# A hybrid transformer kernel on one core: the rotary fold, the first squares and the activation tables of its layer loop are moved

## The reference

```python
for i in range(6):                                   # DEPTH
    x = attn_layer(shift_tokens(x), Wqkv[i], q_scale[i], k_scale[i], Wo[i]) + x
    x = ffn_layer(shift_tokens(x), ln_g[i], ln_b[i], W1[i], b1[i], W2[i], b2[i]) + x

# attn_layer: 16 heads of 64, window 32, on n = 2048 tokens
q = l2norm(q) * qs                                   # divide by the root of the sum of squares
k = l2norm(k) * ksc
q = q * cos * scale + rotate_half(q) * sin * scale   # rotary position tables
k = k * cos * inv + rotate_half(k) * sin * inv
out = local_attention(q, k, v)                       # softmax over 64 keys
# ffn_layer: 128 -> 2 x 341 -> 128
a, gate = jnp.split(xn @ W1 + b1, 2, -1)
return a * jax.nn.gelu(gate, approximate=False) @ W2 + b2
```

## Time and profile before

| | us |
|---|---|
| median of 3 runs | 5192.34 (5176.46 to 5194.83) |
| the profiled execution | 5198.14 |
| its span, first to last instruction | 5196.3 |
| PE busy | 4459.6 (86%) |
| DVE busy | 3876.7 (75%) |
| ACT busy | 3326.2 (64%) |
| POOL busy | 2834.6 (55%) |

### The profile page before, as it was taken

One profiled execution on the slowest core, in us unless ns is written; L12 is line 12 of the kernel. 1 busy time (PEld: TensorE's weight loads), 2 busy tenths in 40 slices (PEclk: granted clock), 3 DMA queues, 4 the chain that ended last, 5 costly groups with the idle time before them and its releaser, 6 DMA issues. The chain is left out here.

```text
span 5196.3 us, 198441 instructions
## 1 busy us (share of the span) xinstructions
PE 4459.6 (86%) x70382; PEld 2776.0 (53%) x70382; DVE 3876.7 (75%) x8099; ACT 3326.2 (64%) x11398; POOL 2834.6 (55%) x2110
## 2 busy tenths in 40 slices
PE   5999999598897988989889756988989889798896
PEld 1333332266565665656656534665656656566565
DVE  7888787387786877868768545877868778687785
ACT  1777777476585775857758413766757667476584
POOL 3000000376675766757667404766757667576674
PEclk6999999899998999999999876999989999899998
DMA  0000000233233232332332302233333322323233
GB/s 13 1 2 2 2 1 1 76 78 86 73 79 87 74 85 76 78 90 73 86 78 78 84 14 86 77 86 78 79 82 79 86 73 77 87 77 85 73 79 97
DMA packets 415347, 340.20 MB, mean 65 GB/s; under 512 B 170607, under 2 KB 312469, under 8 KB 412693
## 3 DMA queue, kind: packets, MB, share of 16 engines
q1 hardware_dynamic: 413972, 332.35, 24.1%
q10 hardware_dynamic: 768, 0.02, 0.0%
HBM read 100.42 MB, written 30.41 MB: 25 GB/s over the span
## 5 line engine op out<-in xcount | busy, mean ns | idle before, releaser
L946 POOL TENSOR_TENSOR g_rn<-g_ss,g_minus_half 128x8 f32<-128x8 f32 x378 | 718.6, 1901 | 394.9 <-DVE g_ss L1151 392.7
L946 POOL TENSOR_TENSOR f_rn<-f_ss,f_minus_half 128x8 f32<-128x8 f32 x378 | 718.3, 1900 | 388.8 <-DVE f_ss L1151 384.3
L427 DVE TENSOR_REDUCE a_maxima<-a_max 128x1 f32<-128x512 f32 x1024 | 651.5, 685 | 150.2 <-PE a_max L541 144.0
L351 ACT ACTIVATE a_pex<-a_scores 128x512 f32<-128x512 f32 x1024 | 531.9, 607 | 162.9 <-PE a_scores L550 162.9
L1014 ACT ACTIVATE f_ex<-f_bank,f_nmx 128x64 f32<-128x64 f32 x1536 | 461.3, 314 | 137.6 <-DVE f_nmx L1144 136.8
L1014 ACT ACTIVATE g_ex<-g_bank,g_nmx 128x64 f32<-128x64 f32 x1536 | 461.4, 314 | 132.2 <-DVE g_nmx L1144 131.4
L951 POOL TENSOR_TENSOR g_qr<-g_t 128x512 f32<-128x512 f32 x384 | 493.3, 1285 | 11.8 <-DVE g_t L1124 11.8
L951 POOL TENSOR_TENSOR f_qr<-f_t 128x512 f32<-128x512 f32 x384 | 492.1, 1282 | 13.0 <-DVE f_t L1124 13.0
L1254 PE MATMUL g_bank<-g_wqkv,g_xT 128*128 128x512 f32 x744 | 437.5, 673 | 69.5 <-DVE g_qh L1138 49.7
L1254 PE MATMUL f_bank<-f_wqkv,f_xT 128*128 128x512 f32 x744 | 431.9, 665 | 71.9 <-DVE f_qh L1138 51.8
L282 POOL COPY a_v_head<-a_v_all 128x128 f32 (+1 forms) x16 | 4.6, 289 | 697.9 <-PE a_sums L559 697.9
(11 more groups left out here) (252 smaller groups left out, 11214.6 us busy)
## 6 DMA issues: line engine op xcount, KB each, us to landing
f_vw<-f_vt SPq DMA_DIRECT2D x576, 128.0 KB
g_vw<-g_vt SPq DMA_DIRECT2D x576, 128.0 KB
f_vw<-f_vt SPq DMA_DIRECT2D x384, 64.0 KB
g_vw<-g_vt SPq DMA_DIRECT2D x384, 64.0 KB
f_wqkv<-in_f_Wqkv_dram SPq DMA_DIRECT2D x7, 1536.0 KB, 8.1
g_wqkv<-in_f_Wqkv_dram SPq DMA_DIRECT2D x7, 1536.0 KB, 7.8
f_xs<-xf SPq DMA_DIRECT2D x196, 32.0 KB, 1.8
g_xs<-xf SPq DMA_DIRECT2D x196, 32.0 KB, 1.8
```

Of the source, the lines that this page charges most:

```text
L351: act.activation(pex[:, kt % 2, i % NG, :], ps_s[i % 3][:], ACT.Exp).then_inc(act_ex, 1)
L427: dve.tensor_reduce(maxima[:, m // 4, m % 4:m % 4 + 1], ps_max[m % 3][:], AX.X, ALU.max).then_inc(dv_max, 1)
L946: pool.tensor_tensor(rn[:, b, :], ss[:, b, :], minus_half[:], ALU.pow).then_inc(pl_rn, 1)
```

## The change

1. `fold_rope` moves from POOL to DVE, as eight instructions of 512 elements each. One stands in each DVE group m = 2 to 9, behind `row_stats` and ahead of `gated`. Before the first layer all eight stand in a row, ahead of the first sum of squares. DVE and SP now wait on DVE's own count.
2. `first_square`, `first_squares` and `first_norms` now do chunks 0 and 1, both before the branch. Chunk 1 is done in group m = 10.
3. A small activation of one column (`table`) with Exp stands as the first ACT instruction of a layer, and one with Gelu in the tail of the attention, at tile 17, chunk 0. The table loads go with them.

```diff
             def tile(L, t, q):            # ACT, DVE and POOL alike
-                    if real(t, c, 0) and not (known and n == 0):
+                    if real(t, c, 0) and not (known and n < 2):
...
-                if m - 2 < 6:             # POOL
-                    if m == 2:
-                        pool.wait_ge(dv_t2, upto(dv_t2, L, STEPS - 1)).then_inc(own["pool"], 1)
-                    fold_rope(L + 1, m - 2)
                 if m == NF + 2:
-                    first_norms(L + 1)
+                    first_norms(L + 1, 0)
+                    first_norms(L + 1, 1)
...
+                if (t, c) == (NT + 1, 0): # ACT, during
+                    act.activation(table[:], ident[:, 0:1], ACT.Gelu).then_inc(act_table, 1)
...
-                if m == NF + 1:           # ACT, group
-                    first_square(L + 1)
+                if m > NF:
+                    first_square(L + 1, m - NF - 1)
...
             with act.Fori(0, DEPTH) as L:
+                act.activation(table[:], ident[:, 0:1], ACT.Exp).then_inc(act_table, 1)
                 act.wait_ge(dv_kzero, upto(dv_kzero, L, -1))
...
+            def fold_rope(n, i):          # DVE
+                kind, part, ts = i // 4, i % 4, slice(i % 2 * (NT // 2), i % 2 * (NT // 2) + NT // 2)
+                dve.wait_ge(ld_scales, upto(ld_scales, n, 0, 32))
+                if part < 2:
+                    whole = qk_scales[:, kind, :].unsqueeze(1).broadcast_to([P, NT // 2, DH])
+                    dve.tensor_tensor(rope[:, 2 * kind, ts, :], rope0[:, 2 * kind, ts, :], whole, ALU.mult).then_inc(dv_rope, 1)
+                else:
+                    halves = qk_scales[:, kind, :].rearrange("p (a b) -> p a b", a=2)[:, ::-1, :]
+                    sl = slice(part % 2 * 32, part % 2 * 32 + 32)
+                    dve.tensor_tensor(rope[:, 2 * kind + 1, :, sl], rope0[:, 2 * kind + 1, :, sl],
+                                      halves[:, part % 2, :].unsqueeze(1).broadcast_to([P, NT, 32]),
+                                      ALU.mult).then_inc(dv_rope, 1)
...
                 if m + 1 < NF:            # DVE, group
                     row_stats(L, m + 1, 1 - q)
+                if m == 2:
+                    dve.wait_ge(dv_t2, upto(dv_t2, L, STEPS - 1)).then_inc(own["dve"], 1)
+                if m - 2 < 8:
+                    fold_rope(L + 1, m - 2)
                 if m - 1 < NF:
                     gated(L, m - 1)
-                if m == NF + 1:
-                    first_squares(L + 1)
+                if m > NF:
+                    first_squares(L + 1, m - NF - 1)
...
             with dve.Fori(0, DEPTH) as L:
-                dve.wait_ge(pl_rope, upto(pl_rope, L, 5)).then_inc(own["dve"], 1)
+                dve.wait_ge(dv_rope, upto(dv_rope, L, 7)).then_inc(own["dve"], 1)
```

More of the change, by code:

```diff
@@ L700, in local_stack @@
         nmx = sb("nmx", [P, 2, 4])
+        table = sb("table", [P, 1])
         ex = sb("ex", [P, 2, 4, KEYS])
@@ L1077, in first_xT, with first_square @@
                 act.copy(xT[:, 0, :], ps_fT[:, 0:P]).then_inc(act_xT, 1)
-            def first_square(L):
-                act.wait_ge(pe_qkv, upto(pe_qkv, L, 0))
-                act.wait_ge(dv_ssq, upto(dv_ssq, L, -2))
-                act.activation(sq[:, 0, :], ps_qk[0][:], ACT.Square).then_inc(act_sq, 1)
+            def first_square(L, n):
+                act.wait_ge(pe_qkv, upto(pe_qkv, L, n))
+                act.wait_ge(dv_ssq, upto(dv_ssq, L, n - 2))
+                act.activation(sq[:, n, :], ps_qk[n][:], ACT.Square).then_inc(act_sq, 1)
             def group(L, m, q):
@@ L1098, in _ @@
             first_xT(0)
-            first_square(0)
+            first_square(0, 0)
+            first_square(0, 1)
             act.wait_ge(zeroed, 5)
```

45 lines of the change are left out of this document (18 added, 27 removed).

## The result

| | before | after |
|---|---|---|
| median, us | 5193.44 (5176.46 to 5194.83) | 5112.62 (5105.75 to 5124.08) |
| profiled execution, us (span) | 5198.14 (5196.3) | 5124.08 (5122.1) |
| granted clock, mean | 0.934 | 0.940 |

The ratio is 0.985, with a 95% interval from 0.983 to 0.988. So the change gains 81 us by the medians and 74 by the profiled executions; the forecast was 54. Two more measurements of the same kernel, told with the experiments, gave 5125.19 and 5117.43, that is 65 and 73 us less than before on their chips. Weighed by the number of executions, the three give a gain of some 72 us.

A forecast was written before the change was run, and what follows sets the result against it. No engine is saturated (PE busy 86%), so each stage's last-ending wait counts. Groups 39, edges 4 and starts 11 sum to 54 us: 5198.1 becomes 5144, or 5138 against the median, range 5105 to 5168.

The forecast's parts named there:

- the rival in which the clock never falls: Behind the stand at m = 3 PE's clock stays fast in every layer: 5115 us, chance 0.22.
- Stalls at m = 6 and 7: Feed-forward groups: normalise pairs held by POOL's fold run freely once it leaves, 1.08 + 0.40 = 1.48 us a layer.
- The fold on DVE in the groups: The 0.6 us fold hides in DVE's 0.75 us wait at m = 3 to 9; at m = 2 it delays 0.6.
- The stall at m = 3: The normalise pair, held by POOL's bias b2, ends at 1625.0 instead of 1625.65: 0.65 us gained, ends 0.5 and 1.25.
- The clock: Behind PE's stand at m = 3 the clock falls in half the layers: 1.1 of 2.2 us gained, ends 0 and 2.2.
- Groups in sum: Feed-forward groups: 3.2 us a layer, 39 us over twelve layers, with ends of 24 and 59.
- The attention: The long middle of the attention keeps its instructions and was taken to run at its old pace.
- Starts: Two stack starts: PE's six us of wait for folds go, the turn of x is next late; 5.5 us each, 11 together.
- Edges: Ten edges between layers: chunk 1 ahead of the branch and the early Exp load gain 0.4 us each, 4 us (-5 to +13).
- The Gelu load: Tail of the attention: the moved load delays the PE and ACT chain, costing 0.6 us a layer, inside the groups' sum.
- The rival of the new wait: POOL's bias hits normalises (0.7 us each) or DVE's fold holds up POOL's variance and root: 5175 us, chance 0.10.
- Slower: The fold on DVE lies on the feed-forward path after all: net 41 us slower, 5233 us, chance 0.05.

The follow-up runs named there:

- the fold alone: Kernel before with only the move of the fold to DVE, without the squares or the small activations: 5123.85 us, ratio 0.987.
- POOL folding out of the way: Kernel before, fold still on POOL but cut into eight products of 512 elements, waiting at m = 2 to 6 for the next group's normalise: 5113.56 us, ratio 0.985.
- the repeats: The changed kernel unchanged, measured again in the second and third set: 5125.19 us (ratio 0.987) and 5117.43 us (ratio 0.986).
- the tables alone: Kernel before with only the two small activations and their Exp and Gelu table loads: 5181.67 us, ratio 0.9984.
- the run without it: Changed kernel without the early Gelu activation, the load back ahead of the first gelu: 5096.59 us, ratio 0.982.
- no fold in the loop: Changed kernel with a wait and signal for each fold but the eight at a stack's start, so its output differs: 5113.17 us, ratio 0.984.
- the fold and the Exp load: Changed kernel without chunk 1's square ahead of the branch and without the Gelu load: 5108.76 us, ratio 0.985.
- The products at m = 3: Changed kernel with four more PE products that nobody reads behind the outputs of m = 2: 5094.86 us, ratio 0.983.
- those at the edge: Changed kernel with two unused PE products ahead of the branch and two between the v products: 5098.98 us, ratio 0.982.
- with the other edits: Fold on DVE, Exp load, no Gelu load, chunk 1's square behind the branch, unused products at m = 3 and at the edge: 5083.83 us, ratio 0.981.

## Why the prediction was right, point by point

The time, 5112.6, lies in the range from 5105 to 5168, 25 us below the forecast of 5138 and next to the rival in which the clock never falls (5115). That it lies next to it is chance: the clock did fall, in 4 to 7 of twelve layers.

- **Stalls at m = 6 and 7: right but for a small part.** 1.36 us a layer by the turns 4 to 7; the forecast was 1.48. It laid both stalls to the fold alone; at m = 7 the bias b2 had a share, and it still holds the pair by 0.14 us on average. The collision is shown by the fold alone, and from the other side by POOL folding out of the way.
- **The fold on DVE in the groups: right.** 0.66 to 0.69 us with 0.20 of wait left (0.68 and 0.1 forecast); turns 4 to 7 are the same without it.
- **The stall at m = 3: right mechanism, too small a size.** The forecast had the pair end at 1625.0 of its sum and PE stand for 2.2 us. The pair took 0.82, and PE stands for 1.80. The sum let POOL's bias hold the pair to the bias's own end and beyond. In the second layer the bias runs from 1603.70 to 1604.42 and the pair from 1603.95 to 1604.77, only 0.23 us longer than an undisturbed one. Turns 0 to 3 gave 1.0 us a layer instead of 0.65 (0.6 and 1.0 in the repeats).
- **The clock: the case was right, its worth too small.** It fell in 4 of 12 layers in the profiled execution, and in 6 and 7 in the two repeats, about half, as forecast. The step that was mis-sized took 2.2 us as the price of a fall and half of it as the gain, 1.1. Before, the turns 3 to 4 took 2.32 us over the 4.62. After, a fall behind the shorter stand costs 1.68. So the gain is 1.76 us in the profiled execution, 1.48 with six falls and 1.34 with seven. In the groups it is the largest error of the sum: 0.66 x 12 = 8 us, or 3 to 5 in the repeats.
- **Groups in sum:** 50 us against 39, and 41 and 43 in the repeats, all inside the bounds of 24 and 59.
- **The attention: put at nothing, and 19 us in the profiles.** This is the largest gap between the sum and the traces. The forecast let the attention run at its old pace and named its pace as a point where it might fail. The fold alone, which changes no instruction of these chunks, shows 14 of the 19 us. The three profiles of the changed kernel agree within 4 us, but of the kernel before there is only one, which may be a long one. The cause stays open.
- **Starts: 15 us against 11.** The folds ended at 992.84 (forecast 992.4). The forecast took the turn of x at about 1000.7 as next late. That turn came at 1000.58, as said, and the product of chunk 2 6.3 us sooner. The first start gained 8.3 us to the scaling of chunk 3, since the product of chunk 3 followed at once, which the forecast didn't count; the second gained 7.1.
- **Edges: 2 us against 4, to chunk 3.** ACT's way through the branch took 2.91 us, at the upper of the two bounds. With the old order of the squares chunk 3 came sooner, at 15.9 instead of 17.5, as the tables alone show, but by chunk 7 nothing of that was left. The first `f_vt` started 4.65 to 5.42 us behind PE's last product, as forecast. Counted to chunk 63, an edge gained 1.7 us; three profiles of the same kernel give 262.6, 263.3 and 263.5.
- **The Gelu load: right sign; the size may be too small.** 0.6 us a layer was in the sum, 7 us in all, and the turns show 6 to 8; the run without it says 26 us (11 to 41). The Trainium skill (ScalarE: Activation LUTs, What ACT_TABLE_LOAD costs) has 1380 ns of drain come on top of a load. The trace shows none on either side of this load: it starts at 1593.35, at once behind a copy that ends at 1593.33, and the small activation starts at 1594.64, at once behind it.
- **The rival of the new wait: seen, but small.** POOL's bias does lie over the normalises at m = 3 and, in some layers, at m = 7, which the forecast named as a sign of being wrong; by the pairs it costs 0.23 and 0.14 us a layer, not 0.7. The fold on DVE holds POOL too: POOL's instruction on the variance, 0.22 us before, takes 0.46 to 0.61 beside the fold. In the second layer it starts at 1602.33 inside the fold and ends at 1602.94, just behind the fold's end. This agrees with the Trainium skill (SBUF — State Buffer, Who interferes with whom), which has the two contend and the later one blocked. The root and bias behind it end later by as much. From m = 3 on they have the air that the forecast named; at m = 2 the delay is 0.38 us of stand (1.80 against 1.42 without folds), together with the fold itself.
- **Slower, and a change that doesn't do what it says:** neither came. The wait ahead of the first `f_ag` covers the fold, and the loads stand where the new order puts them.

So the forecast had the mechanisms of the groups and the starts right, and was cautious in most of its terms. Groups, starts and edges measure 67 us against 54 (some 60 and 63 in the repeats). The 7 us that are left to 74 are the attention (+19), the way to turn 0 (-4) and the linear branch (-8), which no run here explains.

## What to carry to other kernels

- When an instruction suddenly takes several times its usual time, look for the engine whose long instruction ends at the same moment, and move that one by a dependence on the victim. This needs no other engine: here POOL kept the fold, in smaller products that waited for the normalise, and the kernel was as fast as with all three parts of the change.
- An operation that is hidden alone may not be hidden beside another. Two parts of this change wanted the same few us of ACT ahead of the first v copy, and up to chunk 3 the one undid the other. Test parts alone and in pairs, not only the sum, and follow a head start to the end of its stage: this one was gone four chunks later.
- Where PE stands for a short time ahead of dense work, look at the granted clock behind the stand. A few unused products in a place where PE would have stood anyway were worth 20 us (3 to 37) and 25 us (9 to 41) here.

## What the runs showed of the hardware that was not expected

- **The length of a stand and the clock behind it.** Ahead of the turn of m = 3 PE stood for 3.44 us in the kernel before, and the turn behind it was late in 12 of 12 layers. At 1.80 us it was late in 4, 6 and 7 of 12 in three profiles of the same kernel, and in 5 to 7 of 12 in four other kernels with that stand. At 1.42, with no fold in the loop and with POOL folding late, it was late in 0 of 24. PE's work on both sides of the stand is the same in all of them.
- **The way through a loop's branch.** ACT needed 2.61 to 3.38 us over the ten edges of the kernel after, 2.32 to 2.44 with the tables alone and 2.34 to 2.55 with the fold and the Exp load; in the kernel after PE's idle time there was 1.87 to 2.48, and DVE's 2.59 to 3.00. Nothing in the trace says what sets these. With the two unused products ahead of it PE showed 0.59 in the second layer, since it was still at work for most of that time.
- **A small activation** on a column of 128 partitions takes 0.20 us, and the copy behind it starts 0.11 us behind its start (1594.64 and 1594.75).
- **Sizes of gains.** Without the Gelu load the kernel is 26 us faster where the turns explain 6 to 8. The products at m = 3 and those at the edge were worth 20 and 25 us alone, but with the other edits 27 together. The intervals of these differences are 15 to 18 us wide either way; what is behind them is open. A kernel with POOL folding late in the loop and DVE folding at the stack's start, which would join 69 us of the groups with 15 of the starts, wasn't tried.
